# A two-layer block with experts and a selective scan on one core: expert rows scattered into x1 with an adding DMA, eight scan units behind the last tile, gating on VectorE, first maxima ahead of the step sizes

## The reference, cut to what matters

```python
x = x + xattn(layernorm(x), ctx, Wq, bq, Wk, bk)             # softmax(qk) mixes positions of x
x = x + ffn0(layernorm(x), router_w, gate_w, up_w, down_w)   # 16 experts, top 2
x = x + mamba(ctx, layernorm(x), in_w, conv_w, ...)          # scan from ctx, gated by silu(x)
x = x + ffn1(layernorm(x), gate2_w, w1, b1, w2, b2)          # 2 experts of 8, chosen once
# ffn0, per token:   sum over its two experts e of  weight_e * (silu(x @ gate_e) * (x @ up_e)) @ down_e
# mamba, per channel and 16 states:   state = state * exp(dt * A) + (dt * u) * b;   y = sum(state * c)
```

## Time and profile before

| | |
|---|---|
| timed runs (median; lowest, highest) | 1575.12 us; 1571.41, 1581.44 |
| the profiled execution, its span | 1575.32 us, 1573.5 us |
| busy shares of the span | PE 87%, VectorE 59%, POOL 50%, ACT 45% |
| mean granted PE clock | 0.928 of full speed |
| largest shares of the chain that ended last | L1774 22%, L1763 21%, L1318 8%, L745 5%, L1543 3%, L1327 3% |
| DMA | 191.66 MB, mean 122 GB/s over the span |

### The profile page before, as it was taken

The page is one execution under the profiler, slowest core; times in us unless marked ns, Lnnn a source line. Parts: engine busy times, 40 slices in busy tenths (PEclk is TensorE's granted clock), DMA queues, the critical chain, the costliest instruction groups (busy, mean ns, idle before and its releaser), DMA issues.

```text
span 1573.5 us, 18692 instructions
## 1 busy us (share of the span) xinstructions
PE 1373.7 (87%) x6077; PEld 1020.3 (65%) x6077; DVE 933.0 (59%) x1189; ACT 707.3 (45%) x1302; POOL 782.8 (50%) x610
## 2 busy tenths in 40 slices
PE   7977883799898989984467999999999999999998
PEld 4434443566565656652465888878787887878786
DVE  3777778899999999996862142242424133242422
ACT  4435433566766766763243333333333333333332
POOL 0000002888888888885612445454444445444442
PEclk9987985799999999998556999999999999999999
DMA  4311353498897888755647700010001000010000
GB/s 110 109 59 50 109 189 133 149 299 265 272 291 254 275 285 288 229 174 175 187 178 276 257 14 0 0 67 8 6 0 62 7 14 0 0 54 1 0 0 27
DMA packets 78967, 191.66 MB, mean 122 GB/s; under 512 B 11544, under 2 KB 16440, under 8 KB 77872
## 3 DMA queue, kind: packets, MB, share of 16 engines
q1 hardware_dynamic: 65584, 157.19, 30.2%
q0 software_dynamic: 6400, 20.98, 4.2%
q10 hardware_dynamic: 6912, 12.59, 2.2%
HBM read 152.71 MB, written 38.01 MB: 121 GB/s over the span
## 4 chain that ended last, share of the span: by engine, by line
PE 59%; DVE 17%; issue 8%; POOL 7%; ACT 6%; DMA 3%; ACTq 0%; SPq 0%; DVEq 0%; POOLq 0%
PE decay L1774 22%; PE bank L1763 21%; DVE decay L1318 8%; POOL S L745 5%; PE bank L1543 3%; DVE S L1327 3%; PE decay L1502 2%; PE bank L1517 1%; PE bank L1718 1%; ACT decay L937 1%; PE bank L1633 1%; PE bank L1591 1%; POOL Y L788 1%; PE bank L1510 1%; PE decay L1570 1%
## 5 line engine op out<-in xcount | busy, mean ns | idle before, releaser
L1458 DVE CAST HFH<-HF 128x512 fp32r<-128x512 f32 x128 | 59.0, 461 | 498.7 <-ACT HF L1090 498.7
L836 POOL TENSOR_TENSOR W2L<-W2R,W2H 128x512 fp32r<-128x512 f32 x128 | 172.3, 1346 | 350.0 <-ACT W2H L1085 350.0
L745 POOL TENSOR_TENSOR S<-DTU,Bb 128x1024 f32<-128x1024 f32 x128 | 303.2, 2391 | 38.2 <-DVE tile_hot L1304 37.2
L1318 DVE TENSOR_TENSOR_SCAN decay<-decay,S 128x1024 f32<-128x1024 f32 x128 | 292.9, 2288 | 3.8 <-POOL S L745 2.4
L1763 PE MATMUL bank<-XSH,W1H 128*128 128x512 f32 x512 | 203.1, 397 | 5.5 <-POOL W1L L832 4.2
L1774 PE MATMUL decay<-W2H,HFH 128*128 128x512 f32 x512 | 200.6, 392 | 5.3 <-DVE HFL L1460 5.3
L1763 PE MATMUL bank<-XSH,W1L 128*128 128x512 f32 x512 | 202.9, 396 | 0.0
L1763 PE MATMUL bank<-XSL,W1H 128*128 128x512 f32 x512 | 202.3, 395 | 0.2 <-issue 0.2
L1774 PE MATMUL decay<-W2L,HFH 128*128 128x512 f32 x512 | 200.2, 391 | 0.0
L1774 PE MATMUL decay<-W2H,HFL 128*128 128x512 f32 x512 | 200.0, 391 | 0.0
L832 POOL TENSOR_TENSOR W1L<-W1R,W1H 128x512 fp32r<-128x512 f32 x128 | 171.0, 1336 | 49.9 <-ACT W1H L1076 49.9
(11 more groups left out here) (213 smaller groups left out, 2078.7 us busy)
## 6 DMA issues: line engine op xcount, KB each, us to landing
WGU<-in_L_ffn_gate_w SPq DMA_DIRECT2D x48, 384.0 KB, 3.7
WGU<-in_L_ffn_up_w SPq DMA_DIRECT2D x48, 384.0 KB, 4.8
WD<-in_L_ffn_down_w SPq DMA_DIRECT2D x48, 384.0 KB, 4.8
Bb<-bc_rows SPq DMA_DIRECT2D x32, 512.0 KB, 7.8
Cb<-bc_rows SPq DMA_DIRECT2D x32, 512.0 KB, 9.2
expert_rows<-YT ACTq DMA_DIRECT2D x48, 256.0 KB, 4.8
W1R<-in_L_ffn_w SPq DMA_DIRECT2D x6, 1024.0 KB, 13.8
W2R<-in_L_ffn_w SPq DMA_DIRECT2D x6, 1024.0 KB, 14.7
```

Source lines behind the costliest of these rows:

```text
L745: pool.tensor_tensor(S[u % NP][:], DTU[:, ds(b, 1), c, :].to_broadcast([P, PAIR, L]), Bb[j][:], ALU.mult).then_inc(dbu_ready, 1)
L836: pool.tensor_tensor(W2L[f % 2][:], W2R[:, ds(e, 1), f, :].rearrange("p e d -> p (e d)"), W2H[f % 2][:].bitcast(F32), ALU.subtract).then_i ...
L1318: dve.tensor_tensor_scan(flat, flat, S[u % NP][:].rearrange("p i l -> p (i l)"), 0.0, ALU.mult, ALU.add).then_inc(scan_done, 1)
```

## The change

The weighted sum of expert rows moves into DRAM. x1 is stored as rows of `x2_rows`; each slot gets, besides its token, its weight (`slot_w`) and a destination row (`slot_dst`; slots without a token add into a spare row). `copy_y` scales by half the weight, and POOL adds the tile's 128 rows into `x2_rows` by an indirect DMA with an addition (`add_rows`), each after the one before has landed, since two tiles can hold the same token. `expert_rows`, its stores, the 32 gathers, the x1 loads and `add_first`/`add_second` go; four loads of x2 and its statistics stand in their place. `gate_by_up` moves from POOL to VectorE, ahead of the scan that precedes `finish_h`. Eight units (`TAIL`) are kept behind the last tile; the other 112 are cut over the 48 tiles, so two tiles of two units are followed by one of three. In the sequences the first two maxima come ahead of the step sizes of the sequence before, `select` goes beside the mix, and ACT's Ln ahead of the scores. `tile_hot`, twice as wide, lies in c-row buffers 5 to 7, whose first loads come later.

```diff
+TAIL = 8
+LATE = 5
...
-        cuts = [AHEAD + (ALL - AHEAD) * j // SLOT_TILES for j in range(SLOT_TILES + 1)]
+        cuts = [AHEAD + (ALL - AHEAD - TAIL) * j // SLOT_TILES for j in range(SLOT_TILES + 1)] + [ALL]
...
-                sp.dma_start(x1_dram[ds(b * T, T)].rearrange("t p d -> p t d"), X1A[:]).then_inc(x1_stored, DMA)
+                sp.dma_start(x2_rows[ds(b * L, L), :].rearrange("(t p) d -> p t d", p=P), X1A[:]).then_inc(x1_stored, DMA)
...
             load_gate_up(0)
             load_down(0)
+            for j in range(LATE, NP):
+                load_c(0, j)
...
-            sp.wait_ge(yt_stored, SLOT_TILES * DMA + DMA)
+            sp.wait_ge(yt_added, SLOT_TILES * DMA)
             sp.sem_inc(xt3_stored, DMA)
-            load_x1(0)
-            load_x1(1)
+            for b in range(B):
+                load_x2(b)
...
             def gather(j0, n):
                 j = j0 + n
                 pool.wait_ge(xgt_ready, j + 1)
-                pool.tensor_copy(gcol[n % 2][:], slot_tok[:, ds(j, 1)]).then_inc(gcol_ready, 1)
-                wait_apart(pool, gcol_ready, j + 1)
...
+            def add_rows(j):
+                pool.wait_ge(yt_ready, j + 2)
+                if j:
+                    pool.wait_ge(yt_added, j * DMA)
+                pool.indirect_dma_start(out=x2_rows, out_offset=bass.IndirectOffsetOnAxis(ap=slot_dst[:, j:j + 1], axis=0),
+                                        in_=YT[j % 2][:], in_offset=None, compute_op=ALU.add).then_inc(yt_added, DMA)
...
-            pool.wait_ge(same_tile, TOP)
+            pool.wait_ge(same_tile, 2 * TOP)
...
             for j in range(SLOT_TILES):
                 for u in units(j):
                     dbu(*bu(u))
-                gate_by_up(j)
+                if j >= 2:
+                    add_rows(j - 2)
                 if j + 2 < SLOT_TILES:
                     gather(0, j + 2)
+            last = units(SLOT_TILES)
+            for u in last[:2]:
+                dbu(*bu(u))
+            add_rows(SLOT_TILES - 2)
+            dbu(*bu(last[2]))
+            add_rows(SLOT_TILES - 1)
+            for u in last[3:]:
+                dbu(*bu(u))
...
+                act.wait_ge(w_ready, b * 2 + 1)
+                act.activation(DT[:, b], XH[:], ACT.Ln).then_inc(ln_ready, 1)
                 if not last:
                     take_scores(b)
                     copy_xin(b + 1, (0, 1))
-                act.wait_ge(w_ready, b * 2 + 1)
-                act.activation(DT[:, b], XH[:], ACT.Ln).then_inc(ln_ready, 1)
...
-                act.wait_ge(yt_stored, j * DMA + DMA)
-                act.activation(YT[:], DOWN[:], ACT.Copy, scale=0.5).then_inc(yt_ready, 1)
+                if j >= 2:
+                    act.wait_ge(yt_added, j * DMA - DMA)
+                act.activation(YT[n % 2][:], DOWN[:], ACT.Copy, scale=slot_w[:, j:j + 1]).then_inc(yt_ready, 1)
...
             def sequence_dve(b, last):
-                softmax(b)
+                row_max(b, 0)
+                row_max(b, 1)
+                if b:
+                    step_sizes(b - 1)
+                normalize(b, 0)
+                row_max(b, 2)
+                normalize(b, 1)
+                row_max(b, 3)
+                normalize(b, 2)
+                normalize(b, 3)
+                if b:
+                    scaled_inputs(b - 1)
...
                 measure(1)
+                if b:
+                    select(b - 1)
                 add_x(2)
...
                     softplus(b)
-                    step_sizes(b)
-                    select(b)
...
                 dve.tensor_tensor(
+                    weight, same, rwt[:, k, :].rearrange("p (t o) -> p t o", o=1).to_broadcast([P, NT, SLOT_TILES]),
+                    ALU.mult).then_inc(same_tile, 1)
...
-                    dve.tensor_copy(slot_tok[:], TURN[:, 0:SLOT_TILES]).then_inc(slots_ready, 1)
+                    ids = TURN[:, 0:SLOT_TILES]
+                    dve.tensor_scalar(slot_w[:], TURN[:, SLOT_TILES:2 * SLOT_TILES], 0.5, None, ALU.mult)
+                    dve.tensor_scalar(empty[:], ids, 0.0, spare_row[:], ALU.is_equal, ALU.mult)
+                    do(dve.tensor_scalar(tokf[:], ids, -1.0, 0.0, ALU.add, ALU.max))
+                    dve.tensor_copy(slot_tok[:], tokf[:])
+                    do(dve.tensor_tensor(empty[:], empty[:], tokf[:], ALU.add))
+                    dve.tensor_copy(slot_dst[:], empty[:]).then_inc(slots_ready, 1)
+            gate_by_up(0)
             finish_h(0, 0)
             for j in range(SLOT_TILES):
                 for i, u in enumerate(units(j)):
+                    if i == 1 and j + 1 < SLOT_TILES:
+                        gate_by_up(j + 1)
                     scan(*bu(u))
...
-            add_first(0)
-            add_second(0)
-            add_first(1)
+            for u in units(SLOT_TILES):
+                scan(*bu(u))
+                read_out(*bu(u))
+            statistics_x2(0)
+            statistics_x2(1)
             for b in range(B):
                 combine(b)
```

More of the change, by code:

```diff
@@ L20 @@
 WQ = 4
-PAD = 6200
+PAD = 14200
+TAIL = 8
+LATE = 5
 class Steps:
@@ L229, in build_program @@
         XGT = [sb(f, f"XGT{i}", [P, K, P]) for i in range(2)]
-        gcol = [sb(f, f"gcol{i}", [P, 1], I32) for i in range(2)]
         GU = [sb(f, f"GU{i}", [P, 2, F]) for i in range(2)]
         HT = [sb(f, f"HT{i}", [FH, 2, P]) for i in range(2)]
-        YT = sb(f, "YT", [P, DM])
+        YT = [sb(f, f"YT{i}", [P, DM]) for i in range(2)]
         f.close()
@@ L242, in build_program @@
         XT3 = sb(g, "XT3", [P, K, L])
+        logits = sb(g, "logits", [P, NT, E2])
         vare3 = sb(g, "vare3", [P, T])
@@ L369, in build_program @@
         yt_ready = sem("yt_ready")
[L370 to L376, removed]
+        yt_added = sem("yt_added")
+        spare_set = sem("spare_set")
+        x2_loaded = [sem(f"x2_loaded{b}") for b in range(B)]
         var2_ready = sem("var2_ready")
@@ L775, in _ @@
                     dbu(*bu(u))
-                gate_by_up(j)
+                if j >= 2:
+                    add_rows(j - 2)
                 if j + 2 < SLOT_TILES:
                     gather(0, j + 2)
-            def gather_y(b, k, count):
-                if b >= 2 and k == 0:
-                    pool.wait_ge(y_loaded[b % 2], b // 2 * (TOP * T * DMA))
-                pool.tensor_copy(pcol[b % 2][k][:], pos[:, k, b * T:(b + 1) * T]).then_inc(pcol_ready, 1)
-                pool.wait_ge(pcol_ready, count)
-                for t in range(T):
-                    pool.indirect_dma_start(
-                        out=(Y1, Y2)[k][b % 2][:, t, :], out_offset=None, in_=y_dram,
-                        in_offset=bass.IndirectOffsetOnAxis(ap=pcol[b % 2][k][:, t:t + 1], axis=0)).then_inc(y_loaded[b % 2], DMA)
+            last = units(SLOT_TILES)
[6 more added lines that the diff above has]
+                dbu(*bu(u))
             def scale_and_shift(n, var, mean, rs, sh, ready, count, done):
@@ L996, in _ @@
             act.sem_inc(yt_ready, 1)
-            act.sem_inc(yt_stored, DMA)
             copy_xg(0, 0)
@@ L1025, in _ @@
             copy_y(0, SLOT_TILES - 1)
-            store_y(0, SLOT_TILES - 1)
-            for u in units(SLOT_TILES - 2)[-1:] + units(SLOT_TILES - 1):
-                if u % HP == HP - 1:
-                    take(u)
+            before = units(SLOT_TILES - 2)[-1:] + units(SLOT_TILES - 1)
+            for u in units(SLOT_TILES):
+                if u != units(SLOT_TILES)[0]:
+                    decay(*bu(u))
+                for v in before:
+                    if v % HP == HP - 1:
+                        take(v)
+                before = [u]
+            take(ALL - 1)
             def silu_z(b):
@@ L1299, in _ @@
             step_sizes(B - 1)
+            scaled_inputs(B - 1)
+            dve.wait_ge(bc_stored, B * 2 * DMA + DMA)
             for k in range(TOP):
@@ L1702, in _ @@
                 down(0, j)
-            for u in units(SLOT_TILES - 1):
+            for u in units(SLOT_TILES - 1) + units(SLOT_TILES):
                 add_states(*bu(u))
```

183 lines of the change are left out of this document (74 added, 109 removed).

## The result

The changed kernel took 1589.97 us (median of 4 runs, 1587.95 to 1592.53), the kernel before 1574.0 beside it: a ratio of 1.0095 with a 95% interval of 1.0057 to 1.0132. The forecast was 1543, faster, in a range of 1515 to 1590. That the time still lies at the very end of this range is luck: the range was drawn to take in late gathers (1579), not a product that is held up. The profiled execution of the kernel after took 1589.8 us, with a span of 1587.8.

What follows compares the result with a forecast made beforehand. VectorE was taken to bound the scan stage (busy 447.3 of 459.4 us), with PE and POOL close behind. 1575.3 - 21 (sequences) + 2 (routing) + 24 (scan stage) - 37 (drain, combination) = 1543 us; own range 1528 to 1559, with rivals 1515 to 1590.

Steps and rivals of the forecast that it cites:

- late gathers (1579): Rival, scan stage: gathers land 3 us late behind the additions, costing 46 us instead of 10; 1579 us, chance 0.11.
- Sequences (-21): Boundaries between sequences: DTU, `select`, early maxima and an energy wait leave the chain; 7.0 us three times, 21 gained.
- routing (+2): Routing: two more one-hot products of 128x768 precede POOL's first product; 2 us lost.
- Drain and combination (-37): After the last scan: statistics start right at its end, logits 70.5 us later instead of 107.7; 37 us gained.
- The gate product's work (0.35 us, +13.4): Scan stage: `gate_by_up` costs VectorE 0.35 us, 0.28 net of overlap, 48 times: 13.4 us, bounds 5 and 21.
- Its wait (9.5, bounds 0 and 25): Scan stage: `gate_by_up` waits for ACT's copy of gate and up products, 8 us, plus 1.5 for the first tile.
- Additions: Scan stage, POOL's queue: an addition lands in 7 us and issues in 1.02; POOL's tile takes 8.15 us.
- no bound as long as issuing an addition costs what a gather costs: Scan stage: POOL's 8.15 us per tile stays under VectorE's 8.45 on this condition.
- DMAs: Scan stage: gathers come about 0.6 us later behind additions, in 16 places where short tiles follow each other: 10 us.
- the additions did not pace the tiles: Rival, scan stage: each addition waits for the one before to land, ahead of the gathers; slower, 1619 to 1677, chance 0.14.
- waits did not stay away: Rival: no waits in the scan stage and quick rounds in the combination; 1519 us, chance 0.15.
- what would show it: Signs: mixes 51 us apart, `gate_by_up` near 0.35, additions landing near 7; against: scan-stage VectorE idle above 40 us.

Runs made afterwards that it cites:

- experiment 7: Kernel after with the sequences' order put back (step sizes and routing ahead of the maxima, logarithm behind the copies): 1606.8 us, ratio 1.0238 to the kernel before.
- experiment 3: Kernel before with the gate product on VectorE behind the scan, reading PSUM, tanh into SBUF, no copy, no additions: 1592.41 us, ratio 1.0118.
- experiment 6: Kernel after with the gate product's second operand from PSUM, gather ahead of the scatter, and rows written instead of added: 1552.97 us, ratio 0.9869.
- experiment 8: Kernel after, product from PSUM, gather first, product behind the scan: 1558.57 us; second version also tanh into SBUF, no copy, slot tables from PSUM: 1553.33 us.
- experiment 2: Kernel before with only the gate product moved from POOL to VectorE, operands in SBUF, ahead of the scan, no additions: 1623.77 us, ratio 1.0328.
- experiment 4: Kernel after with the gate product back on POOL, ahead of the addition: 1587.12 us, ratio 1.0077 to the kernel before.
- experiment 5: Kernel after with the gather issued ahead of the addition: alone 1818.36 us; together with the gate product's second operand from PSUM 1562.32 us.

## Why the prediction was wrong, point by point

- **Sequences (-21) and routing (+2)**: right in the sum; the first scan came 20.4 us earlier, and undoing the reorder alone cost 18.7 at that point. That leaves 1.7 us gained where 2 were to be lost, which is less than that point differs between profiles (experiment 7); the two added products of the routing take 0.96 us each. At the boundary that was walked, DT starts at 126.59 and the mix at 135.75, 9.2 us later, where it was 18.0; the mixes are 50.3 us apart (51 forecast). VectorE's timeline of the kernel after:

```profile
124.93 0.69 DVE L1115 TENSOR_REDUCE nmax<-bank 128x1 f32<-128x512 f32 x1 [1.58 <-PE bank L1527]
...
126.59 2.29 DVE L1165 TENSOR_TENSOR DT<-RL,DT 128x2048 f32<-128x2048 f32 x1
```

- **Drain and combination (-37)**: right; the statistics of x2 start at 778.20, at the end of the last read-out, and the logits stand 71.9 us later (70.5 forecast).
- **The gate product's work (0.35 us, +13.4)**: this step failed. The prediction put at nothing that the product can be held by POOL's `dbu`. Its price came from two rows of the right size and the wrong neighbours: `finish_h` has an operand in PSUM, and the 128x256 product ran in the routing, where POOL had no products to run. The bounds (0.34 to 0.43) held the work alone. With POOL idle or operands in PSUM it is right (0.351 us; 16.0 us of stage in experiment 3); beside `dbu` it took up to 7.9 us, and its busy time was 43.8 us in place of 17.
- **Its wait (9.5, bounds 0 and 25)**: mis-sized; 27.4 us, in 18 waits. The place one scan early was the point named, and it has the larger part: with the product read from PSUM, 32.5 us of wait stay 21.7 when PE's waits for gathered rows fall from 50 to 8 us (experiment 6), and fall to 9.3 at the later place (experiment 8). The rest goes with the late rows.
- **Additions**: the landing, 6.7 us in the middle of the stage (7 taken), was right, and a gather landed 0.7 us later than before (6.5 against 5.8). The issue was not: 1.60 us, not 1.02, so POOL's tile is 2.33 x 2.42 + 1.60 + 1.00 + 2 x 0.27 = 8.8 us and not 8.15, longer than VectorE's 8.45: the condition "no bound as long as issuing an addition costs what a gather costs" did not hold. DMAs were forecast at 10 us; with gate and slots mended, and the gather issued first, the stage is 493.3 against 475.4 of the kernel before with the same gate, 17.9 us.
- **Rivals**: the additions did not pace the tiles (POOL waited 13.7 us for them), the gather did not land 3 us later, and waits did not stay away. The mechanism that decided was not among the rivals, nor in "what would show it", although that list's `gate_by_up` near 0.35 us is what showed it. Another sign on that list did not come: VectorE's idle time in the stage is 35.8 us (529.80 - 493.98), under the 40 named, since a held operation counts as busy.

If what experiments 2 and 3 show in the kernel before carries over, the 70.4 us are 16.0 of work, 34.8 of hold-up, copy and early place (not separated in the kernel before; in the kernel after the hold-up alone was worth 16.7 of its stage, 529.8 - 513.1), and 19.6 left for additions, late rows, slot tables and tail. This split is an estimate, and the parts don't simply add: with no product on VectorE at all (experiment 4) the stage still loses 70.6 us. That the product was held is shown; how the 70.4 us divide stays open.

The Trainium skill, SBUF — State Buffer, section SBUF: two separate sides, has this rule: VectorE and GpSimd share one pair of SBUF ports as an exclusive lock, and a VectorE operation with two SBUF inputs blocks fully against a GpSimd operation that reads SBUF. The traces agree (0.35 us alone, up to 7.94 beside `dbu`, 0.35 again with one operand in PSUM), except for how long a hold lasts, which the last section takes up; the prediction cited other rules and not this one.

## What to carry to other kernels

Before an operation is moved to VectorE, ask which operands lie in SBUF and what POOL runs at that moment: a duration from a row with a PSUM operand, or from a stretch where POOL is quiet, is no price for it. Leave one operand in PSUM where it is still there. And a group's mean far from its median is the first sign to look for: open the line and lay the long instances beside the other engine's timeline.

## What the runs showed of the hardware that was not expected

- How long the product is held varies. At 287.70 us of the kernel after it got in between two of POOL's products (1.92 us, with 6.5 us of the run left), and in experiment 2 only one of the 48 was held beyond the end of the product in progress (the one of 4.43 us). Where the run directly follows an addition it was as a rule held for all two or three products (6.18 and 8.01 us in experiment 5), although VectorE's record begins 0.3 to 0.8 us ahead of POOL's in these two; once, at 621.41 us of the same run, it got in behind the first (1.68 us). POOL's recorded spans are rough, so what decides stays open.
- A cast with one SBUF operand (L1347, 128x48) took 2.24 us beside `dbu`. The cast ahead of it (L1345), as large and also from SBUF to SBUF, took 0.34, so not each one is held. Written from PSUM, the same two tables took 0.20 and 0.21 us beside `dbu` (the second version of experiment 8). POOL's products hardly suffer (2.417 us against 2.39 before).
- An adding scatter costs POOL 1.60 us to issue where a plain one or a gather costs 1.00; it landed in 6.8 us against 6.0. By the Trainium skill, Collectives: The Full Stack, section The bandwidth ceiling: the fold count and why AG ≠ RS ≠ AR, a collective that adds moves 1.93 times slower than one that copies, since each addition reads two sources. That is a rate of large transfers; for the landing of these 256 KB the runs show 1.13.
